# Router links regrouped in the last mixture of experts, and block sums placed in another layer of the dense MLP

## The reference

```python
def _tlin(x, w, s):
    return jnp.einsum('bsi,oi->bso', x, w) * s
h = jax.nn.silu(_tlin(x, w1_w, w1_s)) * _tlin(x, w2_w, w2_s)
h = jax.nn.gelu(_tlin(h, h1_w, h1_s), approximate=False)
h = jax.nn.gelu(_tlin(h, h2_w, h2_s), approximate=False)
return _tlin(h, w3_w, w3_s)
```

```python
router_logits = x_flat @ router_w + router_b
topk_weights, topk_indices = jax.lax.top_k(router_logits, k=TOP_K)
topk_weights = jax.nn.softmax(topk_weights, axis=-1)
...
activated = jax.nn.silu(ff_gate) * ff_up
ff_out = jax.lax.ragged_dot(activated, we_down, group_sizes)
ff_out = ff_out * sorted_weights[:, None]
```

## Time and profile before

| | before |
|---|---|
| median of 3 runs (lowest, highest) | 1038.51 us (1037.92, 1050.32) |
| the profiled execution: its time, its span | 1041.28 us, 1040.0 us |
| PE busy / DVE busy | 895.1 us (86%) / 662.8 us (64%) |
| ACT busy / POOL busy | 436.6 us (42%) / 440.1 us (42%) |
| mean granted clock of TensorE | 0.924 |
| chain that ended last: PE / DVE / issue / ACT / DMA / POOL | 62% / 17% / 6% / 5% / 5% / 3% |

### The profile page before, as it was taken

One profiled execution on the slowest core, in us unless ns is written; L12 is line 12 of the kernel. 1 busy time (PEld: TensorE's weight loads), 2 busy tenths in 40 slices (PEclk: granted clock), 3 DMA queues, 4 the chain that ended last, 5 costly groups with the idle time before them and its releaser, 6 DMA issues.

```text
span 1040.0 us, 23859 instructions
## 1 busy us (share of the span) xinstructions
PE 895.1 (86%) x8571; PEld 717.7 (69%) x8571; DVE 662.8 (64%) x1737; ACT 436.6 (42%) x872; POOL 440.1 (42%) x722
## 2 busy tenths in 40 slices
PE   2877786999997989898799869999878898988898
PEld 1555675788886768676677648988756777765565
DVE  3788764687687664643466636756777888643665
ACT  0345533433343433332256434566514555555222
POOL 5454444452660536223667453647354544101100
PEclk9988955999999989999699859999999999999999
DMA  4411213121221410001133211122111110001452
GB/s 154 130 59 52 84 35 95 44 66 42 64 64 24 133 53 18 4 0 41 44 89 83 68 41 40 45 57 77 35 52 48 28 30 23 19 3 37 132 174 77
DMA packets 51888, 61.46 MB, mean 59 GB/s; under 512 B 7521, under 2 KB 36993, under 8 KB 51393
## 3 DMA queue, kind: packets, MB, share of 16 engines
q1 hardware_dynamic: 46352, 48.53, 15.7%
q0 software_dynamic: 4992, 10.23, 4.4%
q10 hardware_dynamic: 432, 1.18, 0.3%
HBM read 44.91 MB, written 9.24 MB: 52 GB/s over the span
## 4 chain that ended last, share of the span: by engine, by line
PE 62%; DVE 17%; issue 6%; ACT 5%; DMA 5%; POOL 3%; SPq 2%; POOLq 0%; DVEq 0%; ACTq 0%
PE banks L424 8%; DVE NM L494 6%; PE banks L432 4%; PE bank L186 4%; PE banks L175 4%; PE banks L176 4%; PE banks L177 3%; PE bank L445 3%; PE banks L1850 3%; PE bank L2343 3%; PE banks L1853 3%; PE banks L1852 3%; PE banks L1851 3%; PE bank L2234 2%; ACT EE L468 2%
## 5 line engine op out<-in xcount | busy, mean ns | idle before, releaser
L424 PE MATMUL banks<-KT,QT 31*128 31x128 f32 (+1 forms) x1280 | 145.7, 359 | 56.7 <-DVE NM L494 25.4
L494 DVE TENSOR_REDUCE NM<-banks 128x4 f32<-128x1024 f32 (+1 forms) x112 | 137.0, 1223 | 87.2 <-PE banks L424 85.9
L468 ACT ACTIVATE EE<-banks 128x1024 f32<-128x1024 f32 x112 | 114.9, 1026 | 134.5 <-PE banks L432 134.1
L424 PEld LDWEIGHTS banks<-KT,QT 31*128 31x128 f32 x1280 | 104.1, 208 | 89.8 <-DVE NM L494 38.1
L432 PE MATMUL banks<-QT,KT 32*128 32x128 f32 x1792 | 146.4, 303 | 3.1 <-ACT EE L468 2.8
L1781 POOL DMA_INDIRECT XG<-xn,SL x92 | 89.5, 972 | 95.5 <-PE bank L1820 75.4
L432 PEld LDWEIGHTS banks<-QT,KT 32*128 32x128 f32 x1792 | 120.7, 202 | 6.4 <-ACT EE L468 2.8
L445 PE MATMUL bank<-EE,VV 128*32 128x128 f32 x1792 | 70.3, 292 | 0.0
L1921 ACT ACTIVATE ONE<-CP,EC 128x128 fp32r<-128x128 f32 x92 | 37.0, 402 | 71.5 <-PE bank L2153 52.1
L175 PE MATMUL banks<-HH,W1H 128*128 128x512 f32 x128 | 52.7, 412 | 6.5 <-DVE HH L2784 6.5
L445 PEld LDWEIGHTS bank<-EE,VV 128*32 128x32 f32 x1792 | 47.5, 115 | 12.3 <-issue 5.8
(11 more groups left out here) (434 smaller groups left out, 2422.2 us busy)
## 6 DMA issues: line engine op xcount, KB each, us to landing
RAW<-in_w SPq DMA_DIRECT2D x19, 512.0 KB, 3.8
CBS<-cw SPq DMA_DIRECT2D x32, 256.0 KB, 3.7
ys<-Y SPq DMA_DIRECT2D x92, 64.0 KB
CTX<-in_ctx SPq DMA_DIRECT2D x7, 512.0 KB, 5.9
RAW<-in_w SPq DMA_DIRECT2D x8, 352.0 KB, 3.2
KT<-in_keys SPq DMA_DIRECT2D x8, 256.0 KB, 3.1
KT<-KQ SPq DMA_DIRECT2D x32, 64.0 KB, 1.9
QT<-KQ SPq DMA_DIRECT2D x32, 64.0 KB, 2.0
```

Source lines behind the costliest of these rows:

```text
L424: ins = pe.matmul(out, self.QT[r, b1 % 4, 128 * g:128 * g + 128], moving(r, 128 * g), start=True, stop=True)
L468: act.activation(self.EE[:, b % 2, 2 * p:2 * p + 2, :].rearrange("p i k -> p (i k)"), self.K.SB[:, :], ACT.Exp).then_inc(sig("ee").sem, 1)
L494: dve.tensor_reduce(out, src, AX.X, ALU.max, negate=True).then_inc(sig("m1").sem, 1)
```

## The change

Two tables of order move; no instruction is added or removed.

In the last mixture the 18 router links are put behind four steps (5, 5, 5 and 3 links behind steps 5 to 8) where they stood behind six (3 each, steps 5 to 10). PE's transpose of the weights stands behind step 10, not 12. POOL's power stands behind step 7 in place of 8 (its place among POOL's instructions stays the same). The weighing starts behind step 14, not 13, and the down products behind step 15, not 14, each still two a step until they catch up.

In the dense block the eight sums for groups 2 and 3 leave their places behind tiles 0 and 1. Three of each four are made one group earlier, behind tiles 9 (two) and 10 (one), and the fourth behind tile 0.

```diff
-    LOGITS, LTURN, ROUTE, WEIGHTS = 4, 5, 5, 12
+    LOGITS, LTURN, ROUTE, WEIGHTS = 4, 5, 5, 10
...
-        return max(0, min(2 * (i - 12), i + 1, 32))
+        return max(0, min(2 * (i - 13), i + 1, 32))
...
-        return max(0, min(2 * (i - 13), i - 2, 32))
+        return max(0, min(2 * (i - 14), i - 2, 32))
...
-            if self.ROUTE <= i < self.ROUTE + 6:
-                for r in range(3):
-                    self.dve_route(3 * (i - self.ROUTE) + r, K.PS[5][:, :])
+            if self.ROUTE <= i < self.ROUTE + 4:
+                for r in range(5 * (i - self.ROUTE), min(5 * (i - self.ROUTE) + 5, 18)):
+                    self.dve_route(r, K.PS[5][:, :])
...
-            if i == self.ROUTE + 3:
+            if i == self.ROUTE + 2:
                 self.pool_power()
...
                 if f < NGRP:
-                    if k < 2:
-                        if f >= 2:
-                            self.sums.dve(4 * f + 2 * k)
-                            self.sums.dve(4 * f + 2 * k + 1)
+                    if k == 0 and f >= 2:
+                        self.sums.dve(4 * f + 3)
                     elif k == 2:
                         self.dve_stats1(f)
-                    else:
+                    elif k == 3:
                         F.dve_normal(f, 2 * f - 1, f)
             for a in range(4, 12):
...
+                if f + 1 < NGRP and a in (9, 10):
+                    for i in ((0, 1) if a == 9 else (2,)):
+                        self.sums.dve(4 * f + 4 + i)
```

## The result

| | before | after |
|---|---|---|
| median (lowest, highest), 16 runs each | 1043.35 us (1037.92, 1050.32) | 1034.93 us (1031.92, 1047.52) |
| ratio after / before | | 0.9926, 95% interval 0.9906 to 0.9946 |
| profiled execution: time, span | 1041.28 us, 1040.0 us | 1043.58 us, 1042.3 us |
| mean granted clock in it | 0.924 | 0.918 |

The change makes the kernel 0.74% faster, 7.7 us of the 1043.35 (5.6 to 9.8 by the interval): clear of noise, and within the 2% band. (The medians differ by 8.4 us; I go by the ratio, which leaves out the 1047.52 us of after as a slow execution.) The 16 runs of before include the three that were shown ahead of the prediction, whose median of 1038.51 lay near the lower end of the spread.

A forecast was written before the change was run, and what follows sets the result against it. PE bounds the kernel, so only its stops for DVE or transfers can pay. Dense seams 4.2 plus mixture 3.0 (4.15 at full clock) give 7.2 us: 1038.5 - 7.2 = 1031.3 us, range 1028.8 to 1035.3.

The forecast's parts named there:

- the fall of the clock behind step 10: Mixture: PE's new stop of 2.0 plus 0.2 us drops the clock, cutting the gain from 4.15 to 3.0 us.
- the base: Whole kernel: starting median 1038.5 us, from which 7.2 us is taken to forecast 1031.3 us.
- The two gains at full clock: Dense block seams 1.95 and 2.3 us, sum 4.2 us; last mixture 4.15 us.
- 0.65 us for a sum: Dense block, DVE's chain: three sums fewer at a seam bring what follows 3 x 0.65 = 1.95 us earlier.
- a new wait of PE for XB: Dense block: PE waits for XB before the transposes, which start at about 391.2 in place of 393.15.
- The cover of 0.34 us: Dense block, group 0: DVE finishes the moved sums 0.34 us before tile 11's low part could start, so they cost nothing.
- the rival in which the two hold each other up by over a microsecond: Mixture: raw load and weights' write disturb each other by 1.1 us or more; total gain 4.2 to 6 us; 8%.
- The step on SP's list: Mixture: SP must issue expert 6's raw load first, so the weights' write comes 1.1 us earlier, not 1.81.
- the term of minus 1.1 us: Mixture: the low-clock spell after step 10, which lowers the gain from 4.15 to 3.0 us.
- a rival with 25%: Mixture: the clock holds because the stop splits; gain 4.2 + 4.15 = 8.35 us, time 1030.2 us; 25%.
- The low clock in the dense stretch: Dense block, groups 1 and 2: PE's stops also cost clock, granted 0.81 and 0.91 against 1.00 in group 3.
- My range: Whole kernel: 1028.8 to 1035.3 us, covering the first four cases and a microsecond for bounds not closed.

The follow-up runs named there:

- the later transposes: Changed kernel with PE's XB transposes two products later: 36.20 and 36.17 us from seam to seam, against 37.34 and 37.11; nothing gained in group 0.
- the changed kernel again: The changed kernel, unchanged, run again for its spread: dense stretches 14.50 and 14.29 us, mixture 82.42 us, ratio to before 0.9903.
- the mixture alone: Kernel before with only the change's new mixture order, dense block as before: dense stretches 16.46 and 16.51 us, mixture 82.46 us, ratio 0.9929.
- the two sums: Changed kernel's dense block with two of each four sums early (behind tile 9) and two behind tile 0: stretches 15.15 and 14.93 us.
- the last run: Changed kernel plus no-stop mixture order and later XB transposes, second run: seams 36.24 and 36.20, mixture 81.02, median 1056.34 us, ratio to before 0.9902.

## Why the prediction was wrong, and what of it held

Two steps failed: the fall of the clock behind step 10 ("I take it that it falls after step 10"), which did not come, and the base ("so the median should be 1038.5 - 7.2"), which was 4.8 us too low. The two gains at full clock, which are the mechanism, held.

**The dense block.** Forecast 1.95 and 2.3 us; the profile of after shows 1.93 and 2.23. Each step held: 0.65 us for a sum (0.64 and 0.65 by two sums in place of three), stops of about 1.1 and 1.3 us (1.08 and 1.11), a new wait of PE for XB (0.98 us where 1.2 was expected, and 0.75 in group 2), 0.3 us more in group 2 for a PE that had been late, clock 1.00. The sums in their new place cost 0.07 us (39.85 against 39.78 us from the dense block's first stop to the first GG transposes), and were nearer to costing more than I worked out: group 0's rows in DVE's timeline of after are

```profile
372.39 0.70 DVE L2439 SCALAR_TENSOR_TENSOR X<-GA,WGT,X 128x128 f32<-128x128 f32 x1
...
375.53 0.68 DVE L2785 TENSOR_TENSOR HH<-GG,HH 128x512 fp32r<-128x512 f32 x1
```

with 0.70 us for an instruction that takes 0.35 elsewhere, and the low part of tile 11 at 375.53, where the old schedule with this execution's offset of 1.69 us would have had it at 375.47. The cover of 0.34 us was used up, and tile 10's low part (374.05) came 1.0 us later, not 0.8. The two long instructions, 0.70 us here and 0.58 at 375.03, overlap with a POOL instruction each (372.08 for 0.88 us, 374.81 for 0.66); that this is the cause is not shown. What the used-up cover costs once PE comes earlier, the later transposes showed.

**The mixture, at full clock.** Forecast 4.15 us; the usual execution shows 4.0 (82.4 to 82.6 in five of six profiles with the change's order of the mixture, against 86.4 and 86.5). Rows, less the offset: link 8 at 967.12 as forecast, link 13 at 970.40 for 970.35, OA at 972.17 for 972.08, the write at 973.80 for 973.78, the first broadcast at 976.01 for 975.84 (the write took 2.2 us and not 2.06), the first down product at 980.33 for 980.1. PE's stop in step 10 was 1.77 us for 2.0, and no further 0.2 us stood at the transpose. The raw load ahead of the write took its 2.1 us from issue to landing and the write 2.2, so the rival in which the two hold each other up by over a microsecond did not come. The step on SP's list, by which the write is 1.1 and not 1.8 us earlier, was right, and taking the load out of its way moved the write 0.6 us and the mixture 0.4. Of the 4.0 us, 2.5 are stops (6.72 us of brackets in before, 4.19 in the changed kernel again). The other 1.5 are the low spell behind the stop of 3.85 us, which no longer comes: my sum had them in it, as PE's 986.02 of the earlier trace rows, without naming them.

**The clock in step 10: wrong.** "I take it that it falls after step 10", minus 1.1 us, was the case that I made the likeliest. In its place: the granted clock fell behind this stop in none of the seven profiles that have it, nor behind one of 2.89 us, and the term of minus 1.1 us was nothing. I had drawn a length beyond which the clock falls from a single pair of rows, 1.75 us in group 1 of before; the mixture alone and the two sums show the same stop without a fall, and so does group 2 of before (1.73 us), which I had named myself. What I listed as a rival with 25%, gain 8.35 us, is what happened: 4.16 + 4.0 = 8.2 us by the stretches.

**The low clock in the dense stretch** was also given a price in my reading ("these stops also cost clock"). In group 1 it cost nothing (16.44 us with a long low spell, 16.46 with a shorter one), because XB ends the stretch; in group 2 about 0.3 us, which my sum had.

**The sum.** Forecast 7.2 us, measured 7.7 (5.6 to 9.8) by the ratio, 8.2 by the stretches. The interval holds both, so the ratio can't tell a sum with the clock's term from one without; that 7.2 lies near 7.7 does not speak for the term. The stretches do tell, against it.

**The median: wrong base.** The step "so the median should be 1038.5 - 7.2" took the median of three runs as that of the kernel. Over 16 runs it is 1043.35, and 1034.93 is 3.6 us above my 1031.3, inside the range by 0.4 us only, and that by luck: the upper end had been set for gains that fail, not for a base that is off. Against 1038.51 it is a gain of 3.6 us, half of what I forecast; that difference compares three runs with sixteen, and is no measure of the change. My range had terms for each mechanism and none for the base, although one of those three runs, 1050.32, stood 12 us off.

**The late second broadcast** (the mixture 0.9 us longer in the profile of after) is in none of my terms; it was seen in one profile of six with the change's order of the mixture, and once more, smaller and without a stop of PE, in the last run.

**What stays open.** Why the clock falls after one stop and not after another of the same length. One more row of before bears on it, which the prediction does not weigh:

```profile
952.49 0.66 PE L186 MATMUL bank<-CP,XNB 128*128 128x128 f32 x4 [1.92 <-ACT XNB L981]
```

Behind this stop, at the start of the mixture, the lower level came in all thirteen profiles in which it was 1.90 to 1.94 us long, while 1.77 us in step 10 was followed by it in none of seven. PE had had shorter stops just ahead of the first (0.84, 0.35 and 0.49 us in after, at 951.38, 952.04 and 953.02) and none in the 18 us ahead of the other; whether that makes the difference was not tried. Open also is whether the third pair's low spells come from its own stops alone. No run here was aimed at the third pair.

## What to carry to other kernels

Work that has slack goes behind results that nobody waits for, and before a wait put the products that are already possible: moving sums by one layer gave their full 0.65 us each, and two products ahead of the link that waits for the power took away a stop of 1.8 us. A stop that only moves to the next wait of the same list gives nothing. Follow a transfer's path through the issuing engine's list: the write was ready 0.6 us before an unrelated load let it out. When single executions spread by more than the change is worth, compare like stretches of the profiles, and take the base from many runs before an absolute time is stated.

## What the runs showed of the hardware

Stops of TensorE of nearly the same length (1.74 to 1.76 us, same place, same work around them) were followed by the lower clock in one execution and not in two others. Stops of 2.42 and 2.43 us in the dense block were followed by it in three places of three (before and the mixture alone), and one of 2.89 us in the mixture was not. Executions of the changed kernel ran from 1031.92 to 1047.52 us with mean granted clocks from 0.945 down to 0.913; where they differ is not known, since only one execution of a run has a trace. In the profiles of before and after the clock differed most around 570 to 640 us (0.78 and 0.61). The kernel before had medians of 1043 to 1045 us in three sets of rounds and of 1064 to 1066 in two others, 1044.88 and 1064.34 on one and the same chip, while the ratios to it agreed within their intervals. The second of eight broadcasts issued together landed 3.6 to 4.0 us from its issue in twelve profiles, and 4.2 and 4.8 in two.
